# Feed-forward: VectorE takes the next tile's first third of h directly behind the chain of h, and GpSimd forms the rescaling factors

## What is computed

```
h = layernorm(x) * (1 + cb) + sb                      # 512 columns
gate, y = fp4(h) @ fp4(w_gate).T, fp4(h) @ fp4(w_up).T  # 1408 columns each
x = x + gb * (fp4(silu(gate) * y) @ fp4(w_down).T)    # back to 512 columns
# fp4(v): per block of 16 columns, scale = max|v| / 6,
#         nearest of 0, .5, 1, 1.5, 2, 3, 4, 6, times sign and scale
```

## Time and profile before

| what | value |
|---|---|
| median of 3 runs | 4197.71 us (4187.82 to 4198.38) |
| the profiled execution's own time | 4205.14 us |
| its span, from the first to the last instruction | 4203.3 us |
| mean granted TensorE clock | 0.951 of 2.4 GHz |
| TensorE busy over the span | 3613.2 us, 86% |
| VectorE busy over the span | 3382.1 us, 80% |
| ScalarE busy over the span | 1741.2 us, 41% |
| GpSimd busy over the span | 893.6 us, 21% |
| feed-forward's first tile begins, last store | about 2690 us, 4203 us |

### The profile page before, as it was taken

How to read it: one execution, slowest core, us unless ns; L and a number is a source line. 1 busy time by engine, 2 the same in 40 slices (tenths; PEclk the granted TensorE clock), 3 DMA queues, 4 the chain that set the end, 5 groups by cost and what they waited for, 6 DMA issues and landing times. The chain is left out here.

```text
span 4203.3 us, 151665 instructions
## 1 busy us (share of the span) xinstructions
PE 3613.2 (86%) x64072; PEld 2407.6 (57%) x64072; DVE 3382.1 (80%) x7670; ACT 1741.2 (41%) x3493; POOL 893.6 (21%) x609
## 2 busy tenths in 40 slices
PE   4889888898888998988889864389999999999998
PEld 3767667676676776766767752244444444444443
DVE  4787878877788877887788867688888888888887
ACT  2434434344343443433434413344444444444443
POOL 1122222221222122221222215312121121212121
PEclk7999999999999998999999987599999999999999
DMA  3000010000000000000000021032323323232322
GB/s 116 13 24 28 19 33 18 24 28 19 24 28 24 28 18 24 28 21 31 18 24 28 14 78 63 15 80 71 86 72 82 80 74 80 73 83 71 83 71 72
DMA packets 325484, 195.98 MB, mean 47 GB/s; under 512 B 265152, under 2 KB 265920, under 8 KB 324800
## 3 DMA queue, kind: packets, MB, share of 16 engines
q1 hardware_dynamic: 324800, 186.07, 16.3%
HBM read 89.56 MB, written 33.55 MB: 29 GB/s over the span
## 5 line engine op out<-in xcount | busy, mean ns | idle before, releaser
L1614 PE MATMUL fbank<-gT,xqT 128*128 128x464 f16 (+1 forms) x2304 | 497.6, 367 | 110.9 <-DVE h L1506 89.5
L932 DVE COPY_PREDICATED Am<-pick,banks 128x64 f32<-128x64 uint8 (+2 forms) x1792 | 460.1, 257 | 127.5 <-DVE Am L932 12.4
L764 POOL TENSOR_TENSOR raw_up<-raw_up,raw_gate 128x1024 f32<-128x1024 f32 x128 | 311.8, 2436 | 1085.4 <-DVE raw_up L814 1085.4
L1614 PE MATMUL fbank<-uT,xqT 128*128 128x464 f16 (+1 forms) x2304 | 488.4, 362 | 1.4 <-issue 1.2
L1623 PE MATMUL fbank<-dT,hqT 128*128 128x512 f16 x2112 | 467.9, 380 | 8.0 <-DMA hqT<-hq 8.0
L530 PE MATMUL banks<-raw_up,raw_gate 128*128 128x256 f32 x2048 | 458.5, 382 | 1.9 <-DVE xxx L827 1.8
L1614 PEld LDWEIGHTS fbank<-gT,xqT 128*128 128x128 f16 x2304 | 222.3, 99 | 366.7 <-DVE h L1506 117.5
L530 PEld LDWEIGHTS banks<-raw_up,raw_gate 128*128 128x128 f32 x2048 | 386.4, 191 | 54.0 <-issue 2.1
L1614 PEld LDWEIGHTS fbank<-uT,xqT 128*128 128x128 f16 x2304 | 225.6, 98 | 234.6 <-issue 5.2
L1623 PEld LDWEIGHTS fbank<-dT,hqT 128*128 128x128 f16 x2112 | 206.8, 98 | 256.3 <-DMA hqT<-hq 8.5
L775 POOL TENSOR_TENSOR yrs<-yvar,neg_half 128x32 f32<-128x32 f32 x32 | 174.0, 5437 | 840.9 <-DVE yvar L961 840.9
(11 more groups left out here) (234 smaller groups left out, 7259.0 us busy)
## 6 DMA issues: line engine op xcount, KB each, us to landing
raw_scale<-in_L_attn_x SPq DMA_DIRECT2D x32, 512.0 KB, 3.8
xres<-in_L_attn_x SPq DMA_DIRECT2D x32, 512.0 KB, 3.7
x_after_attention<-xres SPq DMA_DIRECT2D x32, 512.0 KB, 3.6
xl<-x_after_attention SPq DMA_DIRECT2D x64, 256.0 KB, 2.7
xr<-x_after_attention SPq DMA_DIRECT2D x64, 256.0 KB, 2.6
out<-xr SPq DMA_DIRECT2D x64, 256.0 KB, 2.2
raw_gate<-in_L_ffn_w_gate SPq DMA_DIRECT2D x1, 2816.0 KB, 11.4
raw_up<-in_L_ffn_w_up SPq DMA_DIRECT2D x1, 2816.0 KB, 18.4
```

The costliest lines, as they stand in the source:

```text
L764: nc.gpsimd.tensor_tensor(xf[:, j % NXF].rearrange("p g b t -> p (g b) t"), xf[:, j % NXF].rearrange("p g b t -> p (g b) t"), hT[:, :, :, ...
L932: nc.vector.copy_predicated(dst, mask, src).then_inc((done or A_step).sem, 1)
L1614: last = nc.tensor.matmul(GU[2 * pair + t][:, 0:w], xqT[:, u, a, g, :], W[:, b_, g, lo_:hi_], start=(k == 0), stop=(k == 3 * G - 1))
```

## The change

VectorE's program changes its order. Before, in the turn of tile n, it was: dve_xa of n+1, first third of h of n, dve_xq of n+1, second and last third of n, chain of h of n, output of n-1. Now it is: dve_xa of n+1, dve_xq of n+1, second and last third of n, chain of h of n, first third of h of n+1, output of n-1. Tile 0's first third goes ahead of the loop. `und` (L1499) and the output's factor (L1517, now `head`) are formed by GpSimd: `und` at the head of its turn, `head` behind `pool_x` and ahead of the addition of the output.

```diff
-            if scales:
-                scales()
...
-            nc.vector.tensor_scalar(hp[:, u, 3:4], hp[:, u, 2:3], undo[:, 2:3], None, ALU.mult).then_inc(ustep.sem, 1)
-            after(dve, ustep, n)
+            after(dve, head_done, n)
             after(dve, out_done, n - 1)
-            nc.vector.scalar_tensor_tensor(tmpo[:], DN[u][:], hp[:, u, 3:4], row_gb[:, u], ALU.mult, ALU.mult).then_inc(scaled_out.sem, 1)
+            nc.vector.scalar_tensor_tensor(tmpo[:], DN[u][:], head[:, u:u + 1], row_gb[:, u], ALU.mult, ALU.mult).then_inc(scaled_out.sem, 1)
...
             if more:
                 dve_xa(dve, 1 - u, n + 1)
-            if do_m:
-                dve_h(dve, u, n, 0)
-            if more:
                 dve_xq(dve, 1 - u, n + 1)
             if do_m:
                 dve_h(dve, u, n, 1)
                 dve_h(dve, u, n, 2)
                 dve_hq(dve, u, n)
+            if more:
+                dve_h(dve, 1 - u, n + 1, 0)
             if do_out:
                 dve_out(dve, j if u else j - 1, 1 - u, n - 1)
...
+        def pool_und(pool, u, n):
+            after(pool, xstep, n, Q_SCALED + 2)
+            after(pool, sil_done, n - 2)
+            after(pool, h_done, n - 2)
+            nc.gpsimd.tensor_tensor(und[:, u, 0:2], undo[:, 0:2], xp[:, u, 2:3].to_broadcast([P, 2]), ALU.mult).then_inc(und_done.sem, 1)
+
+        def pool_head(pool, u, n):
+            after(pool, hstep, n, Q_SCALED + 2)
+            after(pool, scaled_out, n - 2)
+            nc.gpsimd.tensor_tensor(head[:, u:u + 1], undo[:, 2:3], hp[:, u, 2:3], ALU.mult).then_inc(head_done.sem, 1)
+
         def pool_body(pool, j, u, n, do_m, do_out, more):
+            if more:
+                pool_und(pool, 1 - u, n + 1)
             if two_more(n):
                 pool_x(pool, u, n + 2)
+            if do_m:
+                pool_head(pool, u, n)
             if do_out:
...
                     pool_x(pool, 0, 0)
+                    pool_und(pool, 0, 0)
                     pool_x(pool, 1, 1)
...
                     dve_xq(dve, 0, 0)
+                    dve_h(dve, 0, 0, 0)
```

More of the change, by code:

```diff
@@ L1363, in feed_forward @@
         xr, tmpo = sb("xr", [P, 2, C]), sb("tmpo", [P, C])
-        und = sb("und", [P, 2, 3])
+        und, head = sb("und", [P, 2, 3]), sb("head", [P, 2])
         xl_loaded = [sig(f"xl_loaded{u}", 1, 16) for u in range(2)]
@@ L1417, in divide, with quantise @@
             assert k[0] == Q_SCALED
-        def quantise(dve, n, w, src, m, q, s, s16, s_done, full, full_done, pw, step, grid_done, dst, high, low, freed, scales=None):
+        def quantise(dve, n, w, src, m, q, s, s16, s_done, full, full_done, pw, step, grid_done, dst, high, low, freed):
             blocks, bc, k, link = chain(dve, n, w, step, Q_SCALED)
@@ L1497, in dve_xq @@
             quantise(dve, n, C, hx[:], mx[:], q16x, sx, s16x, xs_done, full_x, xfull_done, xp[:, u], xstep, xgrid_done, xq, xq_done, xlow_done,
-                     lambda: after(dve, xT_landed, n - 1),
-                     lambda: nc.vector.tensor_scalar(und[:, u, 0:2], undo[:, 0:2], xp[:, u, 2:3], None, ALU.mult).then_inc(und_done.sem, 1))
+                     lambda: after(dve, xT_landed, n - 1))
         def dve_h(dve, u, n, s):
@@ L1516, in dve_out @@
             after(dve, down_done, n)
-            nc.vector.tensor_scalar(hp[:, u, 3:4], hp[:, u, 2:3], undo[:, 2:3], None, ALU.mult).then_inc(ustep.sem, 1)
-            after(dve, ustep, n)
+            after(dve, head_done, n)
             after(dve, out_done, n - 1)
-            nc.vector.scalar_tensor_tensor(tmpo[:], DN[u][:], hp[:, u, 3:4], row_gb[:, u], ALU.mult, ALU.mult).then_inc(scaled_out.sem, 1)
-        ustep = sig("ustep", 1)
+            nc.vector.scalar_tensor_tensor(tmpo[:], DN[u][:], head[:, u:u + 1], row_gb[:, u], ALU.mult, ALU.mult).then_inc(scaled_out.sem, 1)
+        head_done = sig("head_done", 1)
         def dve_body(dve, j, u, n, do_m, do_out, more):
```

## The result

The changed kernel takes 4144.36 us (median of 4 runs, 4137.39 to 4149.20), the kernel before 4198.05 (median of 4, 4187.82 to 4213.18). The ratio is 0.9868, with a 95% interval of 0.9833 to 0.9903: 54 us or 1.3% less. I had forecast 4163 us, within 4142 to 4189. The size came out at 54 us where 34 were forecast.

A forecast was written before the change was run, and what follows sets the result against it. Bound: a loop of VectorE's own work plus 4.30 us of ScalarE's queue, TensorE second by 0.3 us. Savings of 23.2 (0.38 a tile) + 5.4 + 3.5 + 2 = 34.1 us off 4197.7 gave about 4163 us, range 4142 to 4189.

The forecast's parts named there:

- The loop is VectorE and ScalarE's queue, TensorE second by 0.3 us: VectorE's own work plus 4.30 us of ScalarE's queue, from L1434 to the last third, sets the period; TensorE close behind.
- The rival that all of TensorE's wait is won: TensorE's wait for the first third was the limit: period 21.7 us, 83 us less in all, 4115; chance 0.06.
- 0.24 for L1517: Taking the output's factor from VectorE saves 0.24 us a tile, from its start to that of L1520, wait included.
- 0.14 for L1499: Taking und from VectorE saves the 0.14 us a tile for which it holds the engine.
- 0.05 for the gap before the first third: The gap between L1416 and the first third on VectorE goes: 0.05 us a tile saved, bounds 0 and 0.10.
- 0.05 for collisions: GpSimd's two new operations may hold VectorE: a cost of 0.05 us a tile for both, range 0 to 0.56.
- The second rival: GpSimd's small operations hold VectorE: milder form 4174, with 0.25 of the forecast's chance; hard form 4195, chance 0.11.
- Three slow laps hidden, 5.4: In 3 of 5 laps TensorE's slow matmuls delay VectorE; TensorE's lead would hide this, 3 x 1.80 = 5.4 us.
- Start and tail: First tiles: 2 us saved, bounds 0 and 3. Last tile: 3.5 of VectorE's 4.00 us wait for its last third goes.
- The lead of 3.5 us: TensorE delivers the last third some 4.5 us ahead of VectorE rather than 0.98.
- The phase slips: Rival: GpSimd's modulation meets L1412 in every tile, 0.54 us each, leaving 4197, the same; chance 0.07.
- the first third comes too early: Rival: VectorE waits for sil before the moved first third; slower from 0.56 us on, 4225 at 1 us; chance 0.05.

The follow-up runs named there:

- e5: The changed kernel with ScalarE's statistics of tile n+2 moved behind sil of the last third: 4096.7 us, ratio 0.9810 to the kernel before.
- e4: The kernel before with only VectorE's changed order, both factors left on VectorE: 4176.5 us, ratio 0.9969.
- e6: The kernel before with ScalarE's statistics of tile n+2 moved behind sil of the last third: 4246.2 us, ratio 1.0172.
- e1: The changed kernel with the output's factor formed by VectorE again right ahead of the output, with its wait: 4166.5 us, ratio 0.9944 to the kernel before.
- e3: The kernel before with only und moved to GpSimd: 4182.0 us, ratio 1.0002.
- e8: The changed kernel with an unused 0.55 us power ahead of each of GpSimd's two new operations: 4126.9 us, ratio 0.9878 to the kernel before.
- e2: The kernel before with only the output's factor moved to GpSimd: 4159.7 us, ratio 0.9929.

## Why the prediction held, and where it fell short

- *The loop is VectorE and ScalarE's queue, TensorE second by 0.3 us.* Right. The 4.30 us stand unchanged in the trace after, and e5, which shortens only that queue, takes the wait away. The rival that all of TensorE's wait is won is refuted by the 4.30 and by e4. For "second by 0.3 us" e6 speaks: its wait fell by 0.3 to 0.4 before TensorE set it.
- *0.24 for L1517.* Right: most of e1's ordinary tiles are 0.25 us longer than those of after, 0.20 in the mean of 55.
- *0.14 for L1499.* Right at the spot, somewhat large in the period: L1426 follows L1425 after 0.20 us where L1429 followed after 0.34. But most of e3's periods are only 0.11 or 0.06 shorter, 0.05 in the mean. In the tiles that gain 0.06, GpSimd's addition holds L1412 for longer, 0.82 us where it took 0.76 before.
- *0.05 for the gap before the first third.* Misread, and half too small. I had found the gap in one tile and "in every other tile" none; the trace of before has it in all 60 tiles of the loop, where the first third starts 0.83 to 0.85 behind L1416. e4 gives 0.10 in most tiles, the upper bound, and 0.05 in the mean because of extra gaps at its tiles 5, 15, 25 and so on. After has such gaps too, 0.33 ahead of L1430 at the tiles 7, 17, 27, with periods of 22.35 for 22.05.
- *0.05 for collisions.* GpSimd's rows are 0.19 as taken, though und starts 0.23 behind L1424 and not 0.15, and L1426 kept 0.24 and 0.27. No cost; e8 finds none even at 0.55. The second rival is out in both forms. The Trainium skill's rule (SBUF — State Buffer, Who interferes with whom), that a VectorE instruction with two SBUF inputs and a GpSimd one that reads SBUF exclude each other, is what the rows of 512 columns show, L1430's 1.36 beside an addition of 1.27, but not what the one-column power shows, beside which L1428, with two SBUF inputs, took its 0.19.
- *Three slow laps hidden, 5.4.* Right in size: the difference between laps 32, 42, 52 and laps 12, 22 is 1.84 us each, 1.80 forecast. e4 alone brings it by hiding slow matmuls, as forecast. In the changed kernel there are none left to hide; TensorE's longest wait for h in the loop is 0.97 us.
- *Start and tail.* 2 + 3.5 forecast, 3.0 + 3.9 measured. The tail's number is luck. I had said that 3.5 of the last tile's wait of 4.00 us would go, but that wait stands as it was. VectorE after, last tile, second and last third; before, they waited 3.24 (at 4170.42) and 4.00:

```profile
4114.77 0.70 DVE L1502 SCALAR_TENSOR_TENSOR h<-fbank,und,sil 128x464 f32<-128x464 f32 x1 [1.57 <-ACT sil L1597]
4119.48 0.70 DVE L1502 SCALAR_TENSOR_TENSOR h<-fbank,und,sil 128x464 f32<-128x464 f32 x1 [4.00 <-ACT sil L1597]
```

What went are 1.7 us of the wait ahead of the second third, 1.3 of tile 62's wait for its last third, and small parts. The lead of 3.5 us was also read a little large: TensorE needs 3253.30 - 3248.43 = 4.87 us for the last third, not 4.72.
- *The phase slips* and *the first third comes too early*: neither happened. VectorE shows no wait ahead of the 480 columns in any lap. But e6 shows that the phase is a real danger, dearer than the 0.54 a tile of that rival.
- **The step that failed is the term of L1517's removal.** I priced it, "from its start to that of L1520 are 0.24 us, wait included", as time on the engine. The wait's other effect, that VectorE's program can't run ahead to the jump, was not in the sum at all. It is worth 12 us: 19.6 less 7.3 in five tiles. The pause of 2.9 us stood in the trace of before, in the very tile of the earlier trace rows; I took it as given. That the median still fell into the stated range is owed to the range's width, not to this sum.

The median moved by 54 us, 5 more than the feed-forward's 48.4; that is inside the interval of the ratio, about 15 us to either side, and the attention half scatters by more than that.

## What to carry to other kernels

A wait on a result that the same engine has only just been ordered to form can cost more than the operation: here the next lap began 3.1 to 3.7 us behind it, and with nothing long in between most of that was idle time. Form such factors early, or on an idle engine, so that the last wait of a lap lies well ahead of its last long operations. And before an edit moves work of GpSimd in time, look up what VectorE does at that moment: an operation of 0.25 us took 1.36 beside one of 1.27.

## What the runs showed of the hardware

- A new lap began 3.1 to 3.7 us behind the last result of its own that VectorE waited for, in all laps of before, after, e1, e2 and e4; the pause was the same 2.9 us in laps of 10 tiles and of 30. The work already handed over runs meanwhile; only the rest is seen as a pause, 2.9, 0.8 to 1.1 or 0.4 to 0.6 us.
- GpSimd's operations of 512 columns and VectorE's of two SBUF inputs, or tensor_scalar, held each other up in both directions: L1430 took 1.36 in place of 0.25 (e6), L1426 0.58 in place of 0.27, and GpSimd's L1542 2.53 in place of 1.27 (e5). GpSimd's one-column power (0.55) held neither VectorE's operations of 32 columns nor its tensor_scalar of 88 (e8).
- After TensorE had idled for 3.1 us, 12 matmuls took 4.21 us in place of 2.52, at a granted clock of 0.54 in the first 2.2 us and 0.65 in the next 2.0, that is, partly at the 1.2 GHz level. The same 4.21 came after 2.3 us in e4 and after 2.2 in e6, but also 2.52 after 2.2 in e6 and, before, after 2.86 (at 3225.43). After the waits of at most 1.0 us in the changed kernel's loop the matmuls were never slow.
